# A graph-attention pair of layers on one core: the adjacency mask is made inside the first layer's block, between the steps of the first batch's preparation

## What is computed

```python
# x (8, 2048, 256) float32, adj (2048, 2048) int32
h = relu(layernorm(x))
# layer 0: attention over chunks of 256 columns, one softmax per chunk
q, k, v = heads(h @ Wq.T + bq), heads(h @ Wk.T + bk), heads(h @ Wv.T + bv)
scores = clip(einsum('bhnd,bhjcd->bhnjc', q, kc) / sqrt(64), -10, 10)
scores = where(adj.reshape(N, 8, 256) == 0, -10, scores)
ctx = einsum('bhnjc,bhjcd->bhnd', softmax(scores, -1), vc)
x = x + layernorm(ctx @ Wo.T + bo + h) * gamma + beta
# layer 1: scores are sums of a source and a target term, softmax over all 2048
h = relu(layernorm(x));  q = heads(h @ W)
e = leaky_relu(e_src[:, :, None] + e_dst[:, None, :]);  e = where(adj > 0, e, -9e15)
out = x + elu(einsum('bijh,bjhd->bihd', softmax(e, axis=2), q))
```

## Time and profile before

| | us |
|---|---|
| median of three runs | 5316.2 (5311.72 to 5316.87) |
| profiled execution | 5312.18 |
| its span, first to last instruction | 5310.4 |
| mask block with its store | 0 to 86.8 of the span |
| first score matmul | 166.45 |
| PE, DVE, ACT, POOL busy | 92%, 71%, 55%, 25% |

### The profile page before, as it was taken

One profiled execution on the slowest core, in us unless ns is written; L12 is line 12 of the kernel. 1 busy time (PEld: TensorE's weight loads), 2 busy tenths in 40 slices (PEclk: granted clock), 3 DMA queues, 4 the chain that ended last, 5 costly groups with the idle time before them and its releaser, 6 DMA issues. The chain is left out here.

```text
span 5310.4 us, 139580 instructions
## 1 busy us (share of the span) xinstructions
PE 4904.6 (92%) x56608; PEld 4439.3 (84%) x56608; DVE 3759.9 (71%) x7147; ACT 2901.6 (55%) x3112; POOL 1333.0 (25%) x1472
## 2 busy tenths in 40 slices
PE   2999999999999999999999999975988988989889
PEld 2889888898899889988989889964988978879889
DVE  3666666666666666666666666655888888888888
ACT  2444444444444444444444444434877877778788
POOL 1243334333243324333434333330000000000000
PEclk7999999999999999999999999997999999999999
DMA  5000000000000000000000000003021121120211
GB/s 192 1 17 9 13 9 17 13 9 9 9 21 9 9 13 17 9 13 9 17 13 9 9 9 13 5 27 118 25 74 60 38 67 53 43 73 25 74 52 35
DMA packets 100028, 164.41 MB, mean 31 GB/s; under 512 B 5088, under 2 KB 91488, under 8 KB 92960
## 3 DMA queue, kind: packets, MB, share of 16 engines
q1 hardware_dynamic: 98464, 144.80, 8.4%
q0 software_dynamic: 896, 10.23, 0.5%
HBM read 112.79 MB, written 38.03 MB: 28 GB/s over the span
## 5 line engine op out<-in xcount | busy, mean ns | idle before, releaser
L573 PEld LDWEIGHTS outs<-v_s,probs 128*128 128x128 f32 x16384 | 1973.6, 192 | 81.5 <-issue 3.3
L573 PE MATMUL outs<-v_s,probs 128*128 128x128 f32 x16384 | 1983.9, 275 | 0.6 <-DVE probs L788 0.6
L661 ACT ACTIVATE slot<-slot,shift 128x1024 f32<-128x1024 f32 x1024 | 1111.4, 1088 | 1429.7 <-PE slot L563 1429.7
L788 DVE SCALAR_TENSOR_TENSOR probs<-slot,bound 128x1024 f32<-128x1024 f32 x1024 | 1250.7, 1224 | 721.8 <-ACT slot L661 709.3
L1346 ACT ACTIVATE cond<-s_all,d_sign 128x1024 bf16<-128x1024 f32 x1024 | 1132.2, 1143 | 281.5 <-DVE u L1507 276.0
L421 POOL TENSOR_TENSOR ctx_sum<-ctx_sum,ctx_part 128x256 f32<-128x256 f32 x896 | 647.8, 729 | 1248.3 <-DVE ctx_part L804 1247.5
L562 PE MATMUL slot<-q_hi,k_hl 128*128 128x512 f32 x2048 | 902.2, 441 | 1.1 <-DVE q_lo L744 1.1
L1507 DVE TENSOR_TENSOR u<-cond,mask 128x1024 f16<-128x1024 bf16 x1024 | 691.3, 683 | 169.5 <-ACT cond L1346 109.0
L1236 PE MATMUL sums<-x_plain,u 128*128 128x65 f16 x16384 | 619.3, 195 | 203.9 <-DVE u L1515 158.9
L1241 PE MATMUL sums<-x_mixed,u 128*128 128x130 f16 x8192 | 801.7, 221 | 4.7 <-issue 4.6
L563 PE MATMUL slot<-q_lo,k_hl 128*128 128x512 f32 x2048 | 801.9, 392 | 0.0
(11 more groups left out here) (130 smaller groups left out, 3829.3 us busy)
## 6 DMA issues: line engine op xcount, KB each, us to landing
s_all<-s_turned SPq DMA_DIRECT2D x32, 1024.0 KB, 4.9
adj_in<-in_adj SPq DMA_DIRECT2D x16, 1024.0 KB, 5.8
xs<-in_x SPq DMA_DIRECT2D x32, 512.0 KB, 4.8
x<-y SPq DMA_DIRECT2D x32, 512.0 KB, 3.3
x_s<-x SPq DMA_DIRECT2D x32, 512.0 KB, 5.9
o_s<-x SPq DMA_DIRECT2D x16, 1024.0 KB, 5.4
out<-o_s SPq DMA_DIRECT2D x16, 1024.0 KB, 5.0
mask_t<-mask SPq DMA_DIRECT2D x1, 4096.0 KB, 11.1
```

Of the source, the lines that this page charges most:

```text
L573: end = nc.tensor.matmul(outs[i % OUTS][:, q, :], probs[:, i % PROBS, r, q * P:(q + 1) * P], v_s[:, c * JC + r, h * E1:h * E1 + P], start= ...
L661: nc.scalar.activation(slot[:, :, :], slot[:, :, :], ACT.Exp, bias=shift[:, 0:1], scale=SCALE).then_inc(act_done, 1)
L788: nc.vector.scalar_tensor_tensor(probs[:, i % PROBS, :, :], spot(kind, "step", s, i)[:, :, :], P_LOW, bound[:, (i // H) % 2, :, :], ALU.ma ...
```

## The change

mask_block is gone, and with it a barrier and the wait for the store's landing. Its work stands in layer0_block, a function mask_tile on each of DVE, PE and ACT. The adjacency tiles go through a ring of three input buffers, which are probs (two) and bound seen as int32; the f16 copies are ctx_part and ctx_sum, the f16 identity is in ctx_t, and the transposes go to the two outs. A tile is transposed and copied in two parts of eight. SP loads two adjacency tiles, then the four strips of x, then the others, then stores the mask; the wait for that store stands at the end of the layer. POOL makes the f16 identity first, then issues the weight DMAs, then makes the other constants. The wait for the weights moves down to just before the keys, and the engines begin once both identities are there (consts_ready 4). mask8 is allocated after the weights instead of ahead of them.

```diff
@@ in build
-    with nc.sbuf_tensor("mask8", [P, NT, N], U8) as mask8:
-        with nc.sbuf_tensor("ident16", [P, P], F16) as ident16:
-            mask_block(nc, adj, ident16, mask8, mask_dram)
-        layer0_block(nc, x, wq_t, bq, wk_t, bk, wv_t, bv, wo_t, bo, gamma, beta, x1, mask8)
+    layer0_block(nc, x, adj, wq_t, bq, wk_t, bk, wv_t, bv, wo_t, bo, gamma, beta, x1, mask_dram)
@@ in layer0_block
+ADJ_RING = 3
+ADJ_PARTS = 2
+MASK_WITH_T = (1, 3)
...
         dve_cell = sb("dve_cell", [P, 1])
+        mask8 = sb("mask8", [P, NT, N], U8)
...
+        adj_in = [probs[:, 0:2, :, :].rearrange("p k r n -> p (k r n)").bitcast(I32),
+                  probs[:, 2:4, :, :].rearrange("p k r n -> p (k r n)").bitcast(I32),
+                  bound[:, :, :, :].rearrange("p k r n -> p (k r n)").bitcast(I32)]
+        adj16 = [ctx_part[:, :, :, :].rearrange("p h q d -> p (h q d)").bitcast(F16),
+                 ctx_sum[:, :, :, :].rearrange("p q h d -> p (q h d)").bitcast(F16)]
+        ident16 = ctx_t[:, 0, 0:P // 2].bitcast(F16)
...
@@ SP
+            def load_adj(m):
+                if m >= ADJ_RING:
+                    sp.wait_ge(adj_cast, m - ADJ_RING + 1)
+                sp.dma_start(adj_in[m % ADJ_RING], adj[m * P:(m + 1) * P, :]).then_inc(adj_loaded[m % ADJ_RING], 16)
+
+            load_adj(0)
+            load_adj(1)
             for s in range(NS):
                 load_strip(0, s)
+            for m in range(2, NT):
+                load_adj(m)
+            sp.wait_ge(mask_written, ADJ_PARTS * NT)
+            sp.dma_start(mask_dram, mask8[:, :, :]).then_inc(mask_stored, 16)
@@ POOL
+            nc.gpsimd.memset(ident16, 0.0).then_inc(consts_ready, 1)
...
+            for dst, src in consts:
+                pool.dma_start(dst, src).then_inc(consts_loaded, 16)
             nc.gpsimd.memset(pool_cell[:, :], 0.0)
...
-            for dst, src in consts:
-                pool.dma_start(dst, src).then_inc(consts_loaded, 16)
-            pool.wait_ge(consts_loaded, 16 * len(consts))
...
             inverse_std(1, slice(0, NT))
+            pool.wait_ge(consts_loaded, 16 * len(consts))
@@ PE
-            pe.wait_ge(consts_ready, 2)
-            pe.wait_ge(consts_loaded, 16 * len(consts))
+            pe.wait_ge(consts_ready, 4)
+
+            def mask_tile(m):
+                pe.wait_ge(adj_cast, m + 1)
+                for part in range(ADJ_PARTS):
+                    n = ADJ_PARTS * m + part
+                    if n >= ADJ_PARTS:
+                        pe.wait_ge(mask_written, n - ADJ_PARTS + 1)
...
+                        last = nc.tensor.transpose(adj_t[part][:, t, :], adj16[m % 2][:, jt * P:(jt + 1) * P], ident16)
+                    last.then_inc(adj_transposed, 1)
...
+            mask_tile(0)
+            mask_tile(1)
             for k in range(T_USES):
                 transposes(hs[:, 2 * k:2 * k + 2, :], k + 1, t_first(k), slots[t_first(k) % SLOTS])
-            for s, hp in k_order():
+                if k in MASK_WITH_T:
+                    mask_tile(2 + MASK_WITH_T.index(k))
+            pe.wait_ge(consts_loaded, 16 * len(consts))
+            for n, (s, hp) in enumerate(k_order()):
                 keys(s, hp, t_first(2 * s + 1), k_first(s, hp), slots[k_first(s, hp) % SLOTS])
+                mask_tile(4 + n)
             for k in range(V_USES):
                 make_values(k, v_first(k), slots[v_first(k) % SLOTS])
+                if 4 + K_USES + k < NT:
+                    mask_tile(4 + K_USES + k)
@@ ACT
+            def mask_tile(m):
+                per = NT // ADJ_PARTS
+                for part in range(ADJ_PARTS):
+                    act.wait_ge(adj_transposed, ADJ_PARTS * m + part + 1)
+                    nc.scalar.activation(mask8[:, part * per:(part + 1) * per, m * P:(m + 1) * P], adj_t[part][:, :, :],
+                                         ACT.Copy).then_inc(mask_written, 1)
...
+            for m in range(4):
+                mask_tile(m)
+            act.wait_ge(consts_loaded, 16 * len(consts))
+            for n, (s, hp) in enumerate(k_order()):
                 keys(s, hp, k_first(s, hp), slots[k_first(s, hp) % SLOTS])
+                mask_tile(4 + n)
+            for m in range(4 + K_USES, NT):
+                mask_tile(m)
@@ DVE
+            def mask_tile(m):
+                dve.wait_ge(adj_loaded[m % ADJ_RING], (m // ADJ_RING + 1) * 16)
+                if m >= 2:
+                    dve.wait_ge(adj_transposed, ADJ_PARTS * (m - 1))
+                nc.vector.tensor_scalar(adj16[m % 2], adj_in[m % ADJ_RING], 0.0, None, ALU.is_gt).then_inc(adj_cast, 1)
```

More of the change, by code:

```diff
@@ L68, in dve_gate @@
     nc.vector.memset(cell[:, 0:1], 0.0)
[L71 to L130, removed]
-                for k in range(2):
-                    act.wait_ge(adj_transposed, m * 2 + k + 2)
-                    nc.scalar.activation(mask8[:, :, bass.ds((m * 2 + k) * P, P)], adj_t[k][:, :, :],
-                                         ACT.Copy).then_inc(mask_written, 1)
@@ L207, with layer0_block @@
 assert BATCH_USES % SLOTS == 0
-def layer0_block(nc, x, wq_t, bq, wk_t, bk, wv_t, bv, wo_t, bo, gamma, beta, x1, mask8):
+ADJ_RING = 3
+ADJ_PARTS = 2
+MASK_WITH_T = (1, 3)
+def layer0_block(nc, x, adj, wq_t, bq, wk_t, bk, wv_t, bv, wo_t, bo, gamma, beta, x1, mask_dram):
     with ExitStack() as ctx:
@@ L261, in layer0_block @@
         outs = [ps(f"outs{k}", [P, IT, P]) for k in range(OUTS)]
+        adj_in = [probs[:, 0:2, :, :].rearrange("p k r n -> p (k r n)").bitcast(I32),
[4 more added lines that the diff above has]
+        ident16 = ctx_t[:, 0, 0:P // 2].bitcast(F16)
+        adj_t = [o[:, :, :].rearrange("p q d -> p (q d)").bitcast(F16).rearrange("p (t n) -> p t n", n=P) for o in outs]
+        adj_loaded = [sem(f"adj_loaded{k}") for k in range(ADJ_RING)]
+        adj_cast = sem("adj_cast")
+        adj_transposed = sem("adj_transposed")
+        mask_written = sem("mask_written")
+        mask_stored = sem("mask_stored")
         consts_loaded = sem("consts_loaded")
@@ L381, in _ @@
             store(B - 1, NS - 1)
+            sp.wait_ge(mask_stored, 16)
             sp.wait_ge(x1_stored, 16 * B * NS + 1)
@@ L385, in _ @@
         def _(pool):
+            nc.gpsimd.memset(ident16, 0.0).then_inc(consts_ready, 1)
+            pool.wait_ge(consts_ready, 1)
+            nc.gpsimd.affine_select(out=ident16, in_=ident16, compare_op=ALU.not_equal, fill=1.0,
+                                    base=0, pattern=[[-1, P]], channel_multiplier=1).then_inc(consts_ready, 1)
+            for dst, src in consts:
+                pool.dma_start(dst, src).then_inc(consts_loaded, 16)
             nc.gpsimd.memset(pool_cell[:, :], 0.0)
@@ L480, in _ @@
             pe.sem_inc(probs_used, PROBS)
-            pe.wait_ge(consts_ready, 2)
-            pe.wait_ge(consts_loaded, 16 * len(consts))
+            pe.wait_ge(consts_ready, 4)
[6 more added lines that the diff above has]
+                    per = NT // ADJ_PARTS
+                    for t in range(per):
+                        jt = part * per + t
+                        last = nc.tensor.transpose(adj_t[part][:, t, :], adj16[m % 2][:, jt * P:(jt + 1) * P], ident16)
+                    last.then_inc(adj_transposed, 1)
             def fill(u):
@@ L628, in _ @@
         def _(act):
-            act.wait_ge(consts_ready, 2)
-            act.wait_ge(consts_loaded, 16 * len(consts))
+            act.wait_ge(consts_ready, 4)
+            def mask_tile(m):
+                per = NT // ADJ_PARTS
+                for part in range(ADJ_PARTS):
+                    act.wait_ge(adj_transposed, ADJ_PARTS * m + part + 1)
+                    nc.scalar.activation(mask8[:, part * per:(part + 1) * per, m * P:(m + 1) * P], adj_t[part][:, :, :],
+                                         ACT.Copy).then_inc(mask_written, 1)
             def keys(s, hp, use, slot):
@@ L689, in _ @@
         def _(dve):
-            dve.wait_ge(consts_ready, 2)
-            dve.wait_ge(consts_loaded, 16 * len(consts))
+            dve.wait_ge(consts_ready, 4)
             dve.sem_inc(x1_stored, 1)
@@ L895, in _ @@
             aggregate(1, slice(0, NT))
+            mask_tile(2)
+            mask_tile(3)
             dve.wait_ge(moments_done, 1)
```

10 lines of the change are left out of this document (8 added, 2 removed).

## The result

| | before | changed |
|---|---|---|
| median, us | 5313.96 (4 runs, 5310.4 to 5316.9) | 5240.78 (4 runs, 5239.9 to 5241.9) |
| profiled execution and its span, us | 5312.2, 5310.4 | 5239.9, 5238.1 |
| first score matmul, us | 166.45 | 102.16 |

The ratio is 0.9863, with a 95% interval of 0.9846 to 0.988: 73.2 us less. The forecast was 5251 us and its range began at 5241, so the sign and most of the size were right, and the measured median lies 0.2 us outside the range. The gain was about 9 us larger than the sum of the prediction (63.6), and it has two parts. All of layer 0 came 64.3 us earlier, as summed. The other 8 us came behind layer 0, in the code of layer 1, which the change doesn't touch, and the second half of the experiments is about them.

The account below looks back on a forecast made before the run. The opening before the first score matmul was taken to count in full; its terms moved that matmul from 166.45 to 102.8 us, 63.6 less, giving 5248.6 or 5252.6 us by baseline; forecast 5251, range 5241 to 5268.

Parts of the forecast that it names:

- Constants, memset, casts: Start of the opening: constants ready at 12.3 us, then DVE's memset (4.3) and two casts (2.5), done at 19.1 us.
- The late start's rival: POOL's weight issues take twice as long beside adjacency loads: 7 us more, 5258 us; chance 0.12.
- x: Landing of x's four strips, behind two adjacency tiles: between 19.1 and 22.5 us, taken as 22.
- POOL's part: POOL's rstd between the statistics of x and normalizing: 3.5 us, with normalizing from 32 us.
- Rounds of keys: Eight rounds of keys, each with a mask tile: 3.7 us a round, sixteen transposes 1.1 us (bounds 0.9 and 1.88).
- POOL's residual (0.5): First rounds of keys: 0.5 us added in all for DVE casting beside POOL's residual work (bounds 0 and 3).
- Values, queries: End of the opening: keys end at 77.1 us, values with four tiles' transposes take 19.2, queries 6.45; first score at 102.8.
- The unloosened chain: Mask tiles still come every 4.35 us, as in the old loop, with 7.5 us a load: 5262 us; chance 0.07.
- Nothing else in the two layers is touched.: Everything behind the first score stays as it was, so the whole gain is the opening's 63.6 us.
- the sign by which to see the error: Whole kernel: the prediction is wrong if the span shrank by another amount than the first score moved.
- The clock in the mask block: Old mask block: the granted clock rose once, at 63 us, after only f16 transposes, so transposes count as work for it.

Follow-up runs that it names:

- b_pe439: Kernel before, with 439 instructions more (878 already satisfied waits) in PE's program at the start of layer 0: 5315.53 us, ratio 1.0003.

## Why the prediction was right where it was, and what it missed

- *Constants, memset, casts.* 12.3 predicted, 12.3 measured (POOL's f32 identity at 12.01 + 0.29). DVE's memset came at 13.64, not 12.5, and its casts ended at 20.2, not 19.1; x landed later still, so this cost nothing. The late start's rival is out: POOL's 13 issues took 9.7 us beside the loads, as before.
- *x.* 22 predicted, 21.84 measured. The upper bound (22.5) had the right neighbour: x beside weights is slow. The strips even took 15.0 to 17.1 us, the last issue waiting until 10.7.
- *POOL's part.* 3.5 predicted, 5.0 measured, with casts beside it. This term was mis-sized by 1.5 us, so normalizing started at 33.55, not 32, and the keys at 48.29, not 47.
- *Rounds of keys.* 3.7 predicted, 3.57 measured; transposes 1.1 predicted, 1.07 measured. The upper bound, 1.88, would have added 6 us (0.4 for each of eight rounds, 0.8 for each of four tiles), so the scaling by the f32 rows carried weight. The clock stood at 1.00 from 48 us on. The Trainium skill, TensorE: Matmul & The Clock Gate, Part 4: PE-mode transpose, says that a transpose doesn't count as PE being busy in the same way and that the full clock doesn't come with it. Here the measurement decides: the granted clock rose from 0.50 at 42 to 46 us to 1.00 at 48 with nothing but transposes on PE. What I had added for POOL's residual (0.5) was about what it took: two casts of 1.38 and 1.67 where the rest took 1.23.
- *Values, queries.* First values 76.89 (77 predicted), first score 102.16 (102.8). The opening was right to 0.7 us, by small errors of both signs.
- *The unloosened chain.* Its price, 7.5 us for a load, was wrong: beside the keys and the values a load took 4.7 to 6.8 us here, and with two buffers the loss was 3.6 us, as much of it through the clock as through the wait.
- *"Nothing else in the two layers is touched."* This step failed, by 8.0 us. The code of layer 1 is untouched, but it stands 439 instructions further on in PE's program, and its six turns came out 6.3 us shorter. b_pe439 shows that this shift alone does it (198.7 us for the six), and the branch records show how: one 16 KB packet of instructions to wait for at a jump and not two. The other 1.7 us, between first score and first store, are chance: the fourteen profiles spread there from 3692.6 to 3698.0 us without order. The prediction had named the sign by which to see the error, a span that shrinks by another amount than the first score moves. It had priced no row for it, though 6.1 to 8.1 us of issue at each turn stood in the trace of the kernel before.
- *The clock in the mask block.* The prediction read one rise there, at 63 us. It stands in the rows, but the column also reads 1.00 up to 50 us, and all sixteen tiles took 1.88 to 1.89 us: the rise came as a tile ended, and PE began the next one at 68.33, when the column read 0.50 again. What the block has is a rise behind transposes, not transposes at the full clock.
- *Against which number.* The sum from the profiled execution was 5248.6 and the median of the three earlier runs led me to 5251. The median of four is 5314.0, 2 us lower, which took another part of the gap.

## What to carry to other kernels

An opening can be summed like a clock, and transposes, casts and copies of a preparation cost little between the uses of another one when each engine has a gap there; but ask of every wait that goes what the transfer behind it will now collide with. Look for idle time that is put down to "issue" at the turns of a long loop, and then for the length of the branch at the loop's line and for packets of instructions beside it: here PE stood still for 6.0 to 8.1 us a turn, and writing the loop out on every engine that turns, not on one, was worth 42 us. An unchanged loop isn't a constant as long as something ahead of it grows, so differences of 0.1 to 0.2% between versions need a look at the turns before they are put down to the edit.

## What I hadn't expected of the hardware

- A jump back in a long loop waits for the instructions to come in. On PE it took 6.6 to 8.5 us in layer 1 and 3.3 to 4.0 in layer 0, but 0.2 us in the short loop of the mask block. In layer 0 PE's matmuls hide it. DVE's own branch takes 0.06 us, but DVE stood still for 3.2 and 2.8 us behind one.
- Where PE's loop stands in its program decides how many 16 KB packets a jump waits for, one or two. That, and the time at the lower clock behind the jump, moved six turns between 196.7 and 208.5 us.
- POOL slows DVE's f32 work and DVE slows POOL's. Normalizing sixteen pieces took 8.62 us beside POOL's residual work and 5.25 us in b_pe439, where POOL waited for the late transposes:

```profile
119.57 5.25 DVE L712 TENSOR_SCALAR hs<-xs,moments,rstd 128x256 f32<-128x256 f32 x16 [3.50 <-POOL rstd L404]
```

- A queue's issues aren't free when the DMA engines are full: SP's four issues of x took 2.1 us before, 9.1 in the changed kernel and 15.4 behind the store of the mask.
- Satisfied waits cost time: 878 of them on PE, two to an instruction, took 47.7 us.
